# Loading the stacks of q and k from the first slot of a window, on counts of their own

## The reference, cut to what matters

```python
xh = x.reshape(b, c, h, he).transpose(0, 2, 1, 3)
qkv = jnp.einsum('bhce,ef->bhcf', xh, Wqkv) + bqkv
q, k, v = jnp.split(qkv, 3, axis=-1)
att = jnp.einsum('bhqe,bhke->bhqk', q, k) / jnp.sqrt(jnp.float32(he))
mask = jnp.tril(jnp.ones((c, c), dtype=att.dtype), k=-1)
att = jax.nn.softmax(att * mask, axis=-1)
out = jnp.einsum('bhqk,bhke->bhqe', att, v)
```

## Time and profile before

| | us |
|---|---|
| median of 3 runs | 3271.78 |
| the runs | 3269.3 to 3272.37 |
| the profiled execution | 3282.02 |
| its span in the trace | 3280.2 |

### The profile page before, as it was taken

How to read it: one execution, slowest core, us unless ns; L and a number is a source line. 1 busy time by engine, 2 the same in 40 slices (tenths; PEclk the granted TensorE clock), 3 DMA queues, 4 the chain that set the end, 5 groups by cost and what they waited for, 6 DMA issues and landing times. The chain is left out here.

```text
span 3280.2 us, 61044 instructions
## 1 busy us (share of the span) xinstructions
PE 2676.9 (82%) x15254; PEld 1546.9 (47%) x15318; DVE 2100.8 (64%) x5668; ACT 1590.0 (48%) x3630; POOL 1728.9 (53%) x3076
## 2 busy tenths in 40 slices
PE   1677777877787778777788699898888988999999
PEld 1223333333333333333333566666666665666666
DVE  3445556555565556555563789898898986555554
ACT  1345455554455445554454055555555554444444
POOL 3563433333343333333333478777777766777766
PEclk7678888888888888888888699999999999999999
DMA  3334233323423233323422200000000000000000
GB/s 52 76 92 56 42 51 58 51 38 52 58 45 51 45 51 55 55 35 55 58 45 71 75 1 1 1 1 1 1 1 1 1 1 9 16 15 16 14 16 18
DMA packets 81303, 113.30 MB, mean 35 GB/s; under 512 B 25100, under 2 KB 37144, under 8 KB 80536
## 3 DMA queue, kind: packets, MB, share of 16 engines
q1 hardware_dynamic: 76360, 101.44, 19.3%
q0 software_dynamic: 3072, 8.39, 0.9%
q10 hardware_dynamic: 1744, 2.16, 0.2%
HBM read 18.98 MB, written 8.39 MB: 8 GB/s over the span
## 5 line engine op out<-in xcount | busy, mean ns | idle before, releaser
L505 ACT ACTIVATE probs<-scoresT 128x512 f32<-128x512 f32 (+3 forms) x1536 | 691.8, 491 | 577.9 <-PE scoresT L648 551.9
L597 DVE TENSOR_REDUCE cand<-ring 128x4 f32<-128x512 f32 x1152 | 717.7, 682 | 295.3 <-PE ring L698 243.9
L425 POOL TENSOR_SCALAR_AFFINE_SELECT probs<-probs 128x128 f32<-128x128 f32 x1024 | 295.5, 298 | 545.2 <-ACT probs L505 540.6
L648 PE MATMUL scoresT<-stage 98*128 98x512 bf16 (+3 forms) x1536 | 495.0, 373 | 96.4 <-ACT probs L505 83.5
L662 PE MATMUL pv<-probs,Vg 128*32 128x512 f32 (+3 forms) x3072 | 321.7, 524 | 38.8 <-POOL probs L425 38.8
L648 PEld LDWEIGHTS scoresT<-stage 98*128 98x128 bf16 x1536 | 127.5, 99 | 395.9 <-ACT probs L505 279.5
L698 PE MATMUL ring<-Km,Qm 64*128 64x512 bf16 (+2 forms) x1792 | 251.6, 324 | 52.6 <-DMA Km<-parts 28.4
L1125 PE MATMUL mm<-w_W,hT 128*128 128x256 f32 x1024 | 255.8, 395 | 9.0 <-ACT z L1213 3.7
L1145 PE MATMUL mm<-w_W,x2T 128*128 128x512 f32 x512 | 244.7, 601 | 0.3 <-DVE x L1364 0.2
L1206 ACT ACTIVATE hT<-mmT,w_be,w_g 128x128 f32<-128x128 f32 x512 | 185.9, 469 | 86.1 <-PE mmT L1136 86.1
L726 PE MATMUL ring<-Vh,upper 128*128 128x128 f32 x256 | 66.8, 353 | 192.3 <-ACT parts L523 192.3
(11 more groups left out here) (254 smaller groups left out, 5446.5 us busy)
## 6 DMA issues: line engine op xcount, KB each, us to landing
stage<-parts SPq DMA_DIRECT2D x256, 96.0 KB
stage<-parts SPq DMA_DIRECT2D x256, 64.0 KB
Qm<-parts SPq DMA_DIRECT2D x128, 128.0 KB
Km<-parts SPq DMA_DIRECT2D x128, 128.0 KB
stage<-parts SPq DMA_DIRECT2D x256, 32.0 KB
out<-result SPq DMA_DIRECT2D x64, 128.0 KB, 1.7
stage<-ct SPq DMA_DIRECT2D x128, 4.0 KB
w_W<-in_W SPq DMA_DIRECT2D x4, 512.0 KB
```

Source lines behind the costliest of these rows:

```text
L425: nc.gpsimd.affine_select(out=d, in_=d, compare_op=ALU.is_gt, fill=0.0, base=0, pattern=[[1, P]], channel_multiplier=-1).then_inc(mask_ok, 1)
L505: nc.scalar.activation(probs[:, n % 8, lo:hi], scoresT[u % SCORE_BANKS][:, lo % 512:(hi - 1) % 512 + 1], ACT.Exp, scale=SOFT).then_inc(exp ...
L597: ins = nc.vector.tensor_reduce(c, src[:].rearrange("p (t a b) -> p t a b", t=c.shape[1], b=P), AX.X, ALU.max)
L648: nc.tensor.matmul(scoresT[u % SCORE_BANKS][:, lo % 512:(hi - 1) % 512 + 1], Ks[0:ROWS, gi, hh, P * kt:P * kt + P], Qs[0:ROWS, gi, hh, lo: ...
```

## The change

The stacks get four semaphores, one per parity for q and for k, in place of one per pair of heads. LOAD stands at slot 0 of both windows and waits only until all scores of the window before are done. It issues the 12 DMAs of q first and then the 12 of k. ACT waits for q's stacks before it evicts the first half of q's projection, and for k's before the first half of k's. PE waits for all of q and all of k of a parity ahead of a window's first score.

In the tables, the last PV of the window before goes from slot 0 to slot 1 (`PV_LAST`), `PV_COPY` from 0 to 2, `EQ` from slot 31 of the window before to slot 4 of its own, `QK` from 8 to 9, `V` in window 0 from 12 to 14, and `PT` in window 1 from 2 to 5.

```diff
-    0: {... "PV_COPY": 0, "TMP": 0, "PT": 5, ... "SUF": 9, "QK": 8, ... "V": 12, "VG": 0, "LOAD": 11, ...
-    1: {"PV_COPY": 0, "TMP": 0, "PT": 2, "WR": 1, "V": 8, "VG": 6, "LOAD": 6, ...
+    0: {... "PV_LAST": 1, "PV_COPY": 2, "EQ": 4, "TMP": 0, "PT": 5, ... "SUF": 9, "QK": 9, ... "V": 14, "VG": 0, "LOAD": 0, ...
+    1: {"PV_LAST": 1, "PV_COPY": 2, "EQ": 4, "TMP": 0, "PT": 5, "WR": 1, "V": 8, "VG": 6, "LOAD": 0, ...
...
-        at(31, ("R", "CT", "dve", PAIRS_MX - 1), ("EQ",))
+        at(31, ("R", "CT", "dve", PAIRS_MX - 1))
+    if scores:
+        at(pos_of["EQ"], ("EQ",))
...
-        stack_in = [sem(f"stack_in{i}") for i in range(PAIRS_MX)]
+        q_in, k_in = ([sem(f"{n}_stack_in{i}") for i in range(2)] for n in "qk")
...
-                                wait_apart(sp, (parts_ok, 4 * (hb + 1 + e[0])), (st_ok, UNITS * (g - 1) + 4 * HPG))
+                                wait_apart(sp, (parts_ok, 4 * (hb + 1 + e[0])), (st_ok, UNITS * (g - 1)))
...
+                            for hh, rows in heads:
+                                put(Qs, hh, 0, 3, parts[rows, 0, 0:3, :], q_in)
+                                put(Qs, hh, 48, 2, parts[rows, 0, 0:2, :], q_in)
+                                put(Qs, hh, 80, 1, parts[rows, 0, 0:1, :], q_in)
+                            for hh, rows in heads:
+                                put(Ks, hh, 0, 3, parts[rows, 1, 0:1, :].broadcast_to([16, 3, S]), k_in)
...
-                                if w == 0 and c == 0:
+                                if c == 0:
                                     act.wait_ge(w_in, 16 * WEIGHTS)
-                                    for s in stack_in:
-                                        wait(act, s, 16 * 12 * 2 * (hb + 1))
+                                    for s in (k_in if w else q_in):
+                                        wait(act, s, 16 * 12 * (hb + 1))
...
+                            if kt == 0 and hh == 0:
+                                pe.wait_ge(q_in[gi], 16 * 12 * (hb + 1))
+                                pe.wait_ge(k_in[gi], 16 * 12 * (hb + 1))
```

More of the change, by code:

```diff
@@ L94 @@
 AT = {
-    0: {"LN_STATS": 1, "LN_NORM": 3, "XT": 6, "PV_COPY": 0, "TMP": 0, "PT": 5, "OT": 21, "WR": 22, "RSUM": 5, "SUF": 9, "QK": 8, "QK_STEP": 2, "MID_LAG": 2, "V": 12, "VG": 0, "LOAD": 11, "MX": 4, "MX_END": 28, "MX_CURVE": 1.1},
-    1: {"PV_COPY": 0, "TMP": 0, "PT": 2, "WR": 1, "V": 8, "VG": 6, "LOAD": 6, "MX": 2, "MX_END": 28, "MX_CURVE": 1.1},
+    0: {"LN_STATS": 1, "LN_NORM": 3, "XT": 6, "PV_LAST": 1, "PV_COPY": 2, "EQ": 4, "TMP": 0, "PT": 5, "OT": 21, "WR": 22, "RSUM": 5, "SUF": 9, "QK": 9, "QK_STEP": 2, "MID_LAG": 2, "V": 14, "VG": 0, "LOAD": 0, "MX": 4, "MX_END": 28, "MX_CURVE": 1.1},
+    1: {"PV_LAST": 1, "PV_COPY": 2, "EQ": 4, "TMP": 0, "PT": 5, "WR": 1, "V": 8, "VG": 6, "LOAD": 0, "MX": 2, "MX_END": 28, "MX_CURVE": 1.1},
     "V_IN": 0, "WR_IN": 1,
 }
-ALONE = {"LN_STATS": 0, "LN_NORM": 1, "XT": 2, "QK": 8, "QK_STEP": 1, "MID_LAG": 1, "V": 12, "PV_COPY": 1, "TMP": 2, "PT": 5, "OT": 11,
+ALONE = {"LN_STATS": 0, "LN_NORM": 1, "XT": 2, "QK": 8, "QK_STEP": 1, "MID_LAG": 1, "V": 12, "PV_LAST": 1, "PV_COPY": 1, "TMP": 2, "PT": 5, "OT": 11,
          "WR": 14, "VG": 14, "LOAD": 14, "MX": 15, "MX_END": 31, "MX_CURVE": 1.0}
@@ L116, in window @@
     if tail:
-        at(pos_of["PV_COPY"], ("PV", -1, 7), ("PV_COPY", -1))
+        at(pos_of["PV_LAST"], ("PV", -1, 7))
+        at(pos_of["PV_COPY"], ("PV_COPY", -1))
         at(pos_of["TMP"], ("TMP", -1))
@@ L335, in run, with put @@
                             if section == "loop":
-                                wait_apart(sp, (parts_ok, 4 * (hb + 1 + e[0])), (st_ok, UNITS * (g - 1) + 4 * HPG))
+                                wait_apart(sp, (parts_ok, 4 * (hb + 1 + e[0])), (st_ok, UNITS * (g - 1)))
                             else:
                                 sp.wait_ge(parts_ok, 4 * (hb + 1 + e[0]))
[L339 to L352, removed]
+                                wait(sp, st_ok, UNITS * (g - 1))
+                            def put(stack, hh, lo, n, src, loaded):
+                                sp.dma_start(stack[lo:lo + 16 * n, par, hh, :], src).then_inc(loaded[par], 16)
+                            heads = [(hh, slice(16 * (HPG * par + hh), 16 * (HPG * par + hh) + 16)) for hh in range(HPG)]
+                            for hh, rows in heads:
[4 more added lines that the diff above has]
+                                put(Ks, hh, 0, 3, parts[rows, 1, 0:1, :].broadcast_to([16, 3, S]), k_in)
+                                put(Ks, hh, 48, 2, parts[rows, 1, 1:2, :].broadcast_to([16, 2, S]), k_in)
+                                put(Ks, hh, 80, 1, parts[rows, 1, 2:3, :], k_in)
                         elif e[1] in ("LOAD_FIRST", "LOAD_MAX"):
@@ L533, in run @@
                         elif kind == "EQ":
-                            g, par = G + 1, (gi + 1) % 2
-                            act.wait_ge(cm_ok, PAIRS_MX * (g + 1))
-                            nc.scalar.activation(eq[:, par], cf[:, par], ACT.Exp, scale=-SOFT).then_inc(eq_ok, 1)
+                            act.wait_ge(cm_ok, PAIRS_MX * (G + 1))
+                            nc.scalar.activation(eq[:, gi], cf[:, gi], ACT.Exp, scale=-SOFT).then_inc(eq_ok, 1)
                         elif kind == "PV_COPY":
@@ L642, in run @@
                             kt, hh = e[2:]
+                            if kt == 0 and hh == 0:
+                                pe.wait_ge(q_in[gi], 16 * 12 * (hb + 1))
+                                pe.wait_ge(k_in[gi], 16 * 12 * (hb + 1))
                             if kt == 0 and hh % 2 == 0:
-                                pe.wait_ge(stack_in[hh // 2], 16 * 12 * (G + 1))
                                 pe.wait_ge(shift_in[hh // 2], 16 * 2 * (G + 1))
```

## The result

The changed kernel takes 3114.65 us (median of 4, 3113.12 to 3119.1) against 3272.07 us for the one before on the same chip: a ratio of 0.9523, 95% interval 0.9506 to 0.9539, 157 us less. The forecast was 3077 us with a range of 3042 to 3112. The direction is right and the stop is gone as forecast, but the gain is 157 us instead of 195, and the time lies 2.7 us outside the range.

The account below looks back on a forecast made before the run. A once-per-pass stop of the whole core, waiting for stack DMAs, was taken as the bound. Per pass 12.95 + 1.5 - 1.4 = 13.05 us, 195 us in all, gave 3077 us, range 3042 to 3112.

Parts of the forecast that it names:

- The stop: Window 0: ACT's wait for stack DMAs goes to zero; PE gains 12.95 us plus 1.5 us of faster clock per pass.
- That the split is worth nothing once LOAD starts early: Window 0: with LOAD starting 14.3 us earlier, the split counts and q-first order, taken alone, are worth nothing.
- The last PV: Start of window 0: the PV one slot later delays VG and so PE by 1.4 us per pass.
- nothing follows in window 1: Window 1: VG stands at slot 6, so the later last PV costs nothing there.
- The rest: Other moved slots in both windows and window 1's LOAD: taken as 0; V and QK bounded at 1 us either way.
- The first rival: Window 0 behind the stop: ACT or POOL becomes bound, 3 to 4 us per pass returned, time 3122; chance 0.10.
- The other term put at 0, window 1: Window 1: the PT and LOAD moves give 0, PT within 0.5 us either way.
- The sum and the reference run: Per pass 13.05 us; 14 loop passes 183, first pass 12, total 195 off the 3271.8 us median.
- DMAs late: Stack DMAs land late in window 0: half the stop stays, 7 us per pass, time 3180; chance 0.04 including no effect.
- The clock: Low clock lasts through window 0: 19 us more against 13 gained, 6 us lost per pass, time 3362; chance 0.03.
- More gained: Low clock at window 0's start ends sooner, PV delay vanishes: 15.5 us per pass, time 3040; chance 0.11.

Follow-up runs that it names:

- e1: The kernel before with LOAD at slot 0 of both windows waiting only for the previous window's scores, EQ at slot 4, no split: 3072.34 us, ratio 0.9391.
- e5: e1 plus the changed kernel's split counts and q-first order: 3084.74 us, ratio 0.9395.
- e6: The changed kernel with LOAD held again until 16 score pieces of its window, split and q-first order kept: 3170.78 us, ratio 0.9654.
- e4: The changed kernel with the last PV and PV_COPY back at slot 0 of both windows: 3092.12 us, ratio 0.9449.
- e12: e5 with PT of window 1 at slot 5 instead of 2, PV_COPY at slot 0: 3073.85 us, ratio 0.9370.
- e9: The changed kernel with QK back from slot 9 to 8 and V left at 14: 3093.74 us, ratio 0.9428.
- e7: e1 with LOAD held until 8 score pieces of its own window are done instead of 0: 3122.0 us, ratio 0.9505.
- e8: The changed kernel with PT of window 1 back from slot 5 to 2: 3152.27 us, ratio 0.9599.
- e11: e5 with QK of window 0 at slot 7 instead of 8: 3098.87 us, ratio 0.9446.

## Why the prediction was right in kind and wrong in size

**The stop.** Right, with its size. The prediction had 12.95 + 1.5 = 14.45 us per pass from the stop and the clock behind it. e1, which carries the early start and hardly more, is 14.6 us ahead at slot 10. The changed kernel is 13.6 us ahead there, with the delay of the last PV already paid. Over the whole pass e1 gains only 13.1 us (182.9 us in 14), since the clock falls once more at slot 19, 1.2 us per pass in the mean. That is a new low stretch, which the changed kernel does not have at this place, and no part of the stop. That e1's total, 3072, lies beside the forecast of 3077 is luck: the forecast had subtracted 1.4 us per pass for the PV, which e1 does not move.

**That the split is worth nothing once LOAD starts early.** Right (e5); that it would be worth much otherwise was not seen (e6).

**The last PV.** The place was right. DVE after, answering to the earlier trace rows:

```profile
687.71 0.43 DVE L585 COPY Vg<-Vh 128x512 f32<-128x512 f32 x1 [2.90 <-PE pv L667]
...
693.95 2.14 DVE L577 TENSOR_SCALAR xn<-h,mv,rstd 128x128 f32 x8 [2.45 <-POOL rstd L437]
```

VG starts 2.8 us after the window's first score (684.88) instead of 1.1, and PE's wait before PT grew from 1.95 to 3.03 us. For window 0 the forecast of 1.4 us was somewhat too high, 0.8 us by e4. But the sentence that nothing follows in window 1 was wrong: 1.1 us more lie there, 1.9 in all. PE waits 0.47 us for ACT, and the first eight WR matmuls then fall into the low clock:

```profile
645.13 1.10 PE L653 MATMUL scoresT<-stage 98*128 98x512 bf16 x2 [0.47 <-ACT probs L509]
646.16 0.65 PE L667 MATMUL pv<-probs,Vg 128*32 128x128 f32 x8
646.74 2.89 PE L749 MATMUL ring<-w_r,OT 128*128 x8
649.46 0.54 PE L653 MATMUL scoresT<-stage 98*128 98x384 bf16 x2
649.85 1.89 PE L749 MATMUL ring<-w_r,OT 128*128 x8
```

Eight take 2.89 us in the low stretch and 1.89 after it. The first eight take 1.9 to 2.0 us in all 14 passes of the kernel before and 2.9 to 3.5 in all of the changed one. In e4, with PV at slot 0, they take 2.0 and 3.3 us in turn, and window 1 follows them, 39.2 and 40.5 us, with the same instructions. In e1 the windows 1 with 3.4 us at 1.2 GHz take 39.9 us (40.1 to 40.2 in e12, which has PT at 5 as well), those with none 38.6 to 39.1; the changed kernel, with 3.4 us, takes 40.8. So of the 1.7 us by which window 1 grew, 0.6 to 0.9 are the order, and about as much is the clock on WR.

**The rest.** This is the step that failed: "V at 14 and QK at 9 move work by one or two slots in a stretch where PE is 87% busy; I bound it at 1 us either way and take 0." QK's slot costs 2 us per pass by e9 (31 us in all, shown by one edit), twice the bound. SUF stands at slot 9 too, and within a slot the list has SUF ahead of QK, so the move by one slot turned their order on PE round: SUF's products (704.98 to 708.40) now stand in front of the projection that ACT waits for. The first rival named the place and the mechanism, ACT's eviction falling into the dense part, and gave it 3 to 4 us and a chance of 0.10; but it was priced as a fate of the removed stop, when it came from the move of QK and was there to be undone. Its sign came true as well, a new wait on the line that was L522 (4.03 us, now L526). To take the densest engine for the bound failed since two engines at 87% and 66%, each waiting for the other at one place, lose time that neither row of busy time shows. EQ costs nothing that shows (e1 has it at slot 4). The other term put at 0, window 1, cost 1.8 us per pass in the mean, as said under the last PV.

**The sum and the reference run.** The forecast per pass was 14.45 for the stop and -1.4 for the PV, 13.05. Measured against the slots it is 14.6 for the stop, -1.0 up to slot 10 for the PV, -2.2 from slot 10 to 20, where QK is, +0.5 at the end of window 0, and -1.8 in window 1: 10.1. The loop so misses 41 us; the first pass gave 15.9 instead of 12, and 38 us remain. Compared by experiments, e4 and e9 give 24 and 31 us, and e1 against the changed kernel 43, which is 12 less than their sum. e1 has the low stretch at slot 19, 1.2 us per pass or 17 us in the loop, and the other three have not; this is enough to explain the overlap. That the 43 us lie near the miss of 38 is chance: some 21 of them, the 1.4 us for the PV in 15 passes, had been forecast, and e1 itself loses 17 us at slot 19.

**The rivals.** DMAs late: e7 makes that case, and the price of 7 us per pass for half a stop is of the right kind (3.8 us at 8 pieces). The clock: PE's clock was not low behind slot 9 of the changed kernel, 1.00 in both stretches; in total there were fewer microseconds at 1.2 GHz, 17.7 per pass after against 30.9 before. A small relative of this rival appears in e1, the 3.4 us at slot 19. More gained: window 0's start has a clock of 0.66 over 20.1 us in both kernels, and the PV delay did not come to nothing. The Trainium skill (TensorE: Matmul & The Clock Gate, A second HAM failure mode: psum-queue depth-cycling) says that short idle times of PE between groups of matmuls can send the clock back and forth. The trace agrees in so far as the clock falls at 686.12, behind idle times of 0.35 and 0.47 us; but this stretch did not grow. The idle time just ahead does not decide it alone: at slot 19 e1 and the kernel before have 1.02 and 1.03 us in front of the same matmul, and the clock falls in one and not in the other. What decides it is not shown.

## What to carry to other kernels

When a transfer is awaited, ask first when it could have started: here that alone took 13 us off a pass, and the split of its count gave nothing on top. When a stall is removed, slots moved along with it must be tried one by one; an instruction of a half-idle engine may be filler exactly where it stands, and one slot later it may be on the path. Look, too, at what already stands in the slot that it moves to: the order inside the slot can be what costs. Moves can hold each other up: undoing PT alone measured worse than leaving PV_COPY and PT both moved or both unmoved.

## What was not expected of the hardware

Pass 0 differs between the sets of runs. Its window 1 took 45.5 to 46.0 us in the trace after and in e1 to e4, and 51.3 to 56.4 in the eight later ones, where the kernel before also measured 3281 to 3284 us instead of 3272. The trace before has 54.6, which is most of the 10 us by which that execution lay above the median of its runs. In this window GpSimd still issues the gathers, and some waits of ACT and DVE end at an event outside the core; which transfer it is was not tried.

The clock need not repeat from pass to pass. In e4 window 1 has 3.4 us at 1.2 GHz in one pass and none in the next, all through the loop, and takes 40.5 and 39.2 us in turn, with the same instructions; e8, e9 and e11 alternate in the same way. A median or a single pass can mislead there: the medians of e4's two windows would give 1.4 us per pass against the changed kernel, where the loop as a whole gives 1.9.
